# First expert product packed by depth, in pairs of blocks

## What is computed

```python
scores = einsum('bsd,de->bse', x, gate_w) + gate_b        # 4 experts
probs = softmax(scores); masked = top-2 of probs, renormalised
h = gelu(einsum('bsd,edh->ebsh', x, w1) + b1)             # 96 -> 384 per expert, exact gelu
y = einsum('ebsh,ehd->ebsd', h, w2) + b2                  # 384 -> 96
out = einsum('bse,ebsd->bsd', masked, y)
x = x + out
```

## Time and profile before

| | us |
|---|---|
| median of 3 runs | 454.79 |
| the runs | 450.12, 454.79, 462.21 |
| span of the profiled execution | 451.7 |
| its own device time | not given; only its span is |
| PE busy | 406.7 (90%) |
| ACT busy | 347.4 (77%) |
| DVE busy | 344.2 (76%) |
| POOL busy | 124.6 (28%) |
| experts' stage, first L1422 to the end of the span | 288.6 to 451.7 |

### The profile page before, as it was taken

How to read it: one execution, slowest core, us unless ns; L and a number is a source line. 1 busy time by engine, 2 the same in 40 slices (tenths; PEclk the granted TensorE clock), 3 DMA queues, 4 the chain that set the end, 5 groups by cost and what they waited for, 6 DMA issues and landing times.

```text
span 451.7 us, 14565 instructions
## 1 busy us (share of the span) xinstructions
PE 406.7 (90%) x5198; PEld 311.8 (69%) x5198; DVE 344.2 (76%) x983; ACT 347.4 (77%) x920; POOL 124.6 (28%) x300
## 2 busy tenths in 40 slices
PE   4658799999999887999999988879999999999995
PEld 2346577777777765777777766668856777777773
DVE  3858788898888976788778886475677877777775
ACT  3548989899899875899999988446786777777773
POOL 5013234434434313334343335186020000000000
PEclk9999999999999999899999998579999999999999
DMA  7310000000000000000000000022002211311300
GB/s 208 73 59 2 2 2 0 0 0 0 0 0 0 2 3 1 3 4 0 0 0 0 0 1 2 1 80 63 0 19 75 87 53 36 89 39 49 87 17 17
DMA packets 7781, 12.15 MB, mean 27 GB/s; under 512 B 2099, under 2 KB 6601, under 8 KB 6982
## 3 DMA queue, kind: packets, MB, share of 16 engines
q1 hardware_dynamic: 7386, 11.60, 9.1%
q0 software_dynamic: 96, 0.07, 0.2%
q10 hardware_dynamic: 268, 0.08, 0.1%
HBM read 10.06 MB, written 1.68 MB: 26 GB/s over the span
## 4 chain that ended last, share of the span: by engine, by line
PE 45%; DVE 27%; ACT 14%; issue 10%; DMA 2%; DVEq 1%; POOL 0%; ACTq 0%; POOLq 0%
PE score_banks L1436 4%; PE score_banks L1433 4%; PE score_banks L1434 4%; DVE negmax L941 3%; PE score_banks L1422 3%; PE score_banks L1423 3%; PE score_banks L1424 3%; ACT qT L898 3%; PE bank L764 2%; ACT kT L899 2%; DVE sumsq L994 2%; PE bank L752 2%; PE score_banks L707 2%; PE bank L810 2%; PE bank L785 2%
## 5 line engine op out<-in xcount | busy, mean ns | idle before, releaser
L1585 DVE TENSOR_TENSOR hidden_lo<-hidden,hidden_hi 128x512 fp32r<-128x512 f32 x96 | 65.7, 686 | 22.6 <-ACT hidden_hi L1489 22.5
L1097 POOL TENSOR_TENSOR stack<-qk,ones 128x192 f16<-128x192 f32 x64 | 32.4, 506 | 152.2 <-DVE qk L1017 84.0
L1487 ACT ACTIVATE hidden<-score_banks 128x512 f32<-128x512 f32 x64 | 38.4, 599 | 24.6 <-PE score_banks L1424 18.8
L752 PEld LDWEIGHTS bank<-vals,probsT 128*64 128x64 f32 (+1 forms) x1536 | 35.1, 126 | 15.0 <-issue 13.3
L820 PE MATMUL score_banks<-perm,probs 128*128 128x128 f32 x288 | 42.5, 275 | 1.6 <-ACT probs L888 1.6
L764 PE MATMUL bank<-w_qkv,xnT 128*128 128x192 f32 x128 | 39.7, 393 | 4.3 <-DVE qk L1017 2.6
L752 PE MATMUL bank<-vals,probsT 128*64 128x18 f32 (+1 forms) x1536 | 41.4, 208 | 1.1 <-DVE x_all L981 0.6
L1436 PE MATMUL score_banks<-hidden_lo,w_hi 128*96 128x512 f32 x96 | 39.0, 406 | 1.9 <-DVE hidden_lo L1585 1.7
L1433 PE MATMUL score_banks<-hidden_hi,w_hi 128*96 128x512 f32 x96 | 39.3, 409 | 0.6 <-ACT hidden_hi L1489 0.6
L1434 PE MATMUL score_banks<-hidden_hi,w_lo 128*96 128x512 f32 x96 | 38.4, 400 | 0.0
L1489 ACT ACTIVATE hidden_hi<-score_banks 128x512 fp32r<-128x512 f32 x64 | 38.0, 593 | 0.0
(11 more groups left out here) (193 smaller groups left out, 1015.7 us busy)
## 6 DMA issues: line engine op xcount, KB each, us to landing
xT_all<-gate_scratch SPq DMA_DIRECT2D x8, 768.0 KB, 5.1
x_all<-in_x SPq DMA_DIRECT2D x4, 384.0 KB, 7.5
out<-moe_final SPq DMA_DIRECT2D x8, 192.0 KB, 2.0
w<-in_w SPq DMA_DIRECT2D x1, 579.0 KB
w<-in_w SPq DMA_DIRECT2D x1, 576.0 KB, 5.3
w_qkv<-in_w_qkv SPq DMA_DIRECT2D x2, 144.0 KB, 6.8
perm<-in_permutations SPq DMA_DIRECT2D x1, 256.0 KB, 2.8
bias_f<-col_scratch SPq DMA_DIRECT2D x8, 12.0 KB
```

The costliest lines, as they stand in the source:

```text
L752: last = pe.matmul(o_bank[rows, pair_of[h2] * 2 * vd:(pair_of[h2] + 1) * 2 * vd], probsT[:, h2, rows], buffer_of(k, odd, -1)[:, w, pair_of ...
L1487: nc.scalar.activation(hidden[m % 2][:], h_bank[m % HBUF], ACT.Gelu)
L1585: v.tensor_tensor(hidden_lo[m % HBUF][:], hidden[m % 2][:], hidden_hi[m % HBUF][:], ALU.subtract).then_inc(q["hidden_lo"], 1)
```

## The change

The three products of a block together sum over 288 rows (96 channels times hi.hi, hi.lo, lo.hi). They are now laid out as two matmuls of 128 rows and a rest of 32 rows. The tiles w1_a, w1_b, w1_c and x_a, x_b, x_c hold the parts stacked on 128 partitions; DMAs between SBUF tiles fill partitions 96 to 127 (pack_weights once, pack_input and pack_last for each chunk, all on SP's queue). Blocks go in pairs: four matmuls of 128 rows, then the two rests, one on partitions 64 to 95 and one on 96 to 127, into two PSUM banks, then pe_second of the two blocks of the pair before. The bias b1 moves from the 97th row into the GELU's bias operand. There are four hidden banks. DVE's steps are put in a new order by hand (dve_first_chunk, dve_chunk): the accumulation of expert 2 moves into the next chunk, the inputs' subtractions come after dve_low of the same block. The transposed gates get a PSUM place of their own, inputs use bank 2 from chunk 1 on, small result tiles now lie in the memory of w1 and w2, and PE's program is straight code for all chunks.

```diff
@@ build: tiles
-        w1_hi, w1_lo = (sb("w1_" + n, [K1, EXPERTS * HID], F32R) for n in ("hi", "lo"))
+        w1_a, w1_b, w1_c = (sb("w1_" + n, [P, EXPERTS * HID], F32R) for n in "abc")
-        moe_hi, moe_lo = (sb("moe_" + n, [K1, CHUNKS, CHUNK], F32R) for n in ("hi", "lo"))
+        moe_a, moe_b = (sb("moe_" + n, [P, CHUNKS, CHUNK], F32R) for n in "ab")
+        moe_c = sb("moe_c", [P, 2, CHUNK], F32R)
@@ experts
-    HBUF = 3
-    LAG = 2
+    HBUF = 4
+    PAIRS = NH // 2
+    THIRD = C // 3
-    h_bank = [score_banks[0][:, 0, :], score_banks[0][:, 1, :], bank[3][:]]
+    h_bank = [score_banks[0][:, 0, :], score_banks[0][:, 1, :], bank[0][:], bank[3][:]]
-    x_bank = [bank[0], bank[2]] + [bank[0]] * (CHUNKS - 2)
+    x_bank = [bank[0]] + [bank[2]] * (CHUNKS - 1)
+    gates_T_ps = g_bank[:, P:2 * P]
     def pe_first(pe, c, m):
-        w = slice(m * P, (m + 1) * P)
-        pe.matmul(h_bank[m % HBUF], w1_hi[:, w], xT_hi[:, c, :], start=True, stop=False)
-        pe.matmul(h_bank[m % HBUF], w1_hi[:, w], xT_lo[:, c, :], start=False, stop=False)
-        pe.matmul(h_bank[m % HBUF], w1_lo[:, w], xT_hi[:, c, :], start=False, stop=True).then_inc(q["hidden_ps"], 1)
+        w, h = slice(m * P, (m + 1) * P), h_bank[m % HBUF]
+        pe.matmul(h, w1_a[:, w], x_a[:, c, :], start=True, stop=False, skip_group_check=True)
+        pe.matmul(h, w1_b[:, w], x_b[:, c, :], start=False, stop=False, skip_group_check=True)
+
+    def pe_rest(pe, c, j):
+
+        for m, x, first in ((2 * j, x_a[:, c, :], 2 * THIRD), (2 * j + 1, x_c[:, c % 2, :], 3 * THIRD)):
+            rows, w = slice(first, first + THIRD), slice(m * P, (m + 1) * P)
+            pe.matmul(h_bank[m % HBUF], w1_c[rows, w], x[rows, :], start=False, stop=True,
+                      skip_group_check=True).then_inc(q["hidden_ps"], 1)
     def pe_chunk(pe, c, k, tail=None, attention_done=None):
-        for m in range(NH):
-            ...
+        for j in range(PAIRS):
+            if j == 0:
+                pe.wait_ge(q["x_packed"], PACKS * (c + 1))
+                pe.wait_ge(x_last_packed[c % 2], 16 * (c // 2 + 1))
+            if is_chunk(c, 0) and j == 0:
+                tail(0)
+            pe_first(pe, c, 2 * j)
+            if is_chunk(c, 0) and j == 0:
+                tail(1)
+            if is_chunk(c, 0) and j == 1:
+                pe_second(pe, 0, 0)
+                pe.wait_ge(attention_done, B)
+            pe_first(pe, c, 2 * j + 1)
+            pe_rest(pe, c, j)
+            if is_chunk(c, 0) and j == 0:
+                tail(2)
+            if inputs_at(c, j) is not None:
+                pe_inputs(pe, inputs_at(c, j))
+            if gates_at(c, j) is not None:
+                pe_gates(pe, gates_at(c, j))
+            if j == 2 and not is_chunk(c, 0):
+                pe_output(pe, c - 1, 1 - k)
+            if is_chunk(c, 1) and j == 5:
+                pe_gates_T(pe, 1)
+            for m in (2 * j - 2, 2 * j - 1):
+                if m >= 0 and not (is_chunk(c, 0) and m == 0):
+                    pe_second(pe, c, m)
+                elif m < 0 and not is_chunk(c, 0):
+                    pe_second(pe, c - 1, NH + m)
+            if is_chunk(c, 0) and j == 1:
+                pe_gates_T(pe, 0)
     def act_chunk(act, c, k):
-            nc.scalar.activation(hidden[m % 2][:], h_bank[m % HBUF], ACT.Gelu)
+            nc.scalar.activation(hidden[m % 2][:], h_bank[m % HBUF], ACT.Gelu, bias=b1_cols[:, m:m + 1])
             at_least(act, q["hidden_used"], G + 1 - HBUF)
-            nc.scalar.activation(hidden_hi[m % HBUF][:], h_bank[m % HBUF], ACT.Gelu).then_inc(q["hidden_hi"], 1)
+            nc.scalar.activation(hidden_hi[m % HBUF][:], h_bank[m % HBUF], ACT.Gelu,
+                                 bias=b1_cols[:, m:m + 1]).then_inc(q["hidden_hi"], 1)
...
+    def pack_weights(sp):
+
+        sp.wait_ge(s["layers"][0]["q"]["w1_split"], 1 + MIDDLE)
+        wa, wb, wc = (w[:].bitcast(F32) for w in (w1_a, w1_b, w1_c))
+        sp.dma_start(wb[0:C, :], wa[0:C, :]).then_inc(q["w1_packed"], 16)
+        sp.dma_start(wb[C:P, :], wc[0:THIRD, :]).then_inc(q["w1_packed"], 16)
+        sp.dma_start(wa[C:P, :], wc[THIRD:2 * THIRD, :]).then_inc(q["w1_packed"], 16)
+        sp.dma_start(wc[C:P, :], wc[2 * THIRD:C, :]).then_inc(q["w1_packed"], 16)
+
+    def pack_input(sp, c):
+
+        sp.wait_ge(q["xhi_ready"], c + 1)
+        at_least(sp, q["x_packed"], PACKS * c)
+        high = x_a[:].bitcast(F32)
+        sp.dma_start(x_b[:].bitcast(F32)[C:P, c, :], high[0:THIRD, c, :]).then_inc(q["x_packed"], 16)
+        sp.dma_start(high[C:P, c, :], high[THIRD:2 * THIRD, c, :]).then_inc(q["x_packed"], 16)
+
+    def pack_last(sp, c, k):
+
+        at_least(sp, q["hidden_ps"], NH * (c - 1))
+        sp.dma_start(x_c[:].bitcast(F32)[C:P, k, :],
+                     x_a[:].bitcast(F32)[2 * THIRD:C, c, :]).then_inc(x_last_packed[k], 16)
+
     def sync_program(sp):
+        pack_weights(sp)
+        for c in range(2):
+            pack_input(sp, c)
+            pack_last(sp, c, c)
         store_gates(sp, 0)
         load_spread(sp, 0, 0)
         load_spread(sp, 1, 1)
+        for c in range(2, CHUNKS):
+            pack_input(sp, c)
+        pack_last(sp, 2, 0)
         store_output(sp, 0, 0)
         store_gates(sp, 1)
         load_spread(sp, 2, 0)
+        pack_last(sp, 3, 1)
...
     def pe_program(pe, tail, attention_done):
-        pe.wait_ge(s["w1_loaded"], 16 * 2)
+        pe.wait_ge(q["w1_packed"], 16 * 4)
         pe_chunk(pe, 0, 0, tail, attention_done)
-        for c in range(1, 4):
+        pe_chunk(pe, 1, 1)
+        for c in range(2, CHUNKS):
             pe_chunk(pe, c, c % 2)
-        with pe.Fori(2, CHUNKS // 2) as cc:
-            pe_chunk(pe, 2 * cc, 0)
-            pe_chunk(pe, 2 * cc + 1, 1)
-        for m in range(NH - LAG, NH):
+        for m in range(NH - 2, NH):
             pe_second(pe, CHUNKS - 1, m)
         pe_output(pe, CHUNKS - 1, 1)
```

More of the change, by code:

```diff
@@ L128, in build @@
         layers = [attention(nc, sb, sem, s, layer) for layer in range(2)]
+        s["layers"] = layers
         whole_program(nc, s, setup, layers, experts(nc, sb, sem, s, out))
@@ L665, in attention @@
              "stat_ready", "ln_step", "ln_logged", "ln_guessed", "ln_newton_step", "w1_split", "w2_split")
-    q = {n: sem(n + L) for n in names}
+    only = (("xn_ready", "xnT_ps", "ln_step", "ln_logged", "ln_guessed", "ln_newton_step"),
+            ("squares_ready", "squares_summed", "sumsq_ready", "log_ready", "guess_ready", "newton_step", "rnorm_ready",
+             "row_group_done", "probsT_copied_b", "w1_split", "w2_split"))
+    q = {n: sem(n + L) for n in names if n not in only[layer]}
     def on(n):
@@ L1344, in experts @@
     xT = s["moe_xT"]
-    weighted = sb("moe_weighted", [C, CHUNK])
-    acc = [sb(f"acc{k}", [C, CHUNK]) for k in range(2)]
-    final = [sb(f"moe_final{k}", [P, CT, C]) for k in range(2)]
+    weighted = s["w1"][:, 0:CHUNK]
+    acc = [s["w1"][:, (1 + k) * CHUNK:(2 + k) * CHUNK] for k in range(2)]
+    final = [s["w2"][:, k * CT:(k + 1) * CT, :] for k in range(2)]
     gates = sb("gates", [P, UNITS, EXPERTS])
@@ L1373, in experts @@
     q = {n: sem("moe_" + n) for n in names}
+    x_last_packed = [sem(f"moe_x_last_packed{k}") for k in range(2)]
     spread_loaded = [sem(f"moe_spread_loaded{k}") for k in range(2)]
@@ L1376, in experts, with inputs_at, gates_at @@
     GSTEPS = 7
-    def inputs_at(c, m):
-        if is_chunk(c, 0) and m in (2, 4, 6, 8, 10):
-            return 1 + m // 2
-        return 7 if is_chunk(c, 1) and m == 0 else None
-    def gates_at(c, m):
-        if is_chunk(c, 0) and m in (4, 6, 8, 10):
-            return m // 2
-        return {0: 6, 2: 7}.get(m) if is_chunk(c, 1) else None
+    PACKS = 16 * 2
+    def inputs_at(c, j):
+        if is_chunk(c, 0) and j > 0:
+            return 1 + j
+        return 7 if is_chunk(c, 1) and j == 0 else None
+    def gates_at(c, j):
+        if is_chunk(c, 0) and j > 1:
+            return j
+        return {0: 6, 1: 7}.get(j) if is_chunk(c, 1) else None
     def pe_inputs(pe, c):
@@ new lines, in dve_first_chunk @@
+    def dve_first_chunk(v, last_statistics):
+        dve_low(v, 0, 0)
+        last_statistics()
+        rank_first(v)
+        dve_low(v, 0, 1)
+        dve_select(v, 0)
+        dve_renormalise(v, 0)
+        dve_low(v, 0, 2)
+        dve_inputs(v, 2)
+        dve_gates_T(v, 0)
+        dve_low(v, 0, 3)
+        dve_low(v, 0, 4)
+        dve_inputs(v, 3)
+        dve_low(v, 0, 5)
+        norm_root(v, s, q, 1)
+        dve_low(v, 0, 6)
+        dve_inputs(v, 4)
+        dve_weigh(v, 0, 0, 0)
+        dve_low(v, 0, 7)
+        dve_low(v, 0, 8)
+        dve_inputs(v, 5)
+        dve_weigh(v, 0, 0, 1)
+        dve_low(v, 0, 9)
+        dve_accumulate(v, 0, 0, 1)
+        dve_low(v, 0, 10)
+        dve_inputs(v, 6)
+        dve_weigh(v, 0, 0, 2)
+        dve_low(v, 0, 11)
@@ new lines, in dve_chunk @@
+    def dve_chunk(v, c, k):
+        dve_accumulate(v, c - 1, 1 - k, 2)
```

(36 more changed lines are left out.)

106 lines of the change are left out of this document (24 added, 82 removed).

## The result

The changed kernel took **459.13 us** (median of 21 runs, 456.65 to 470.22), the kernel before 455.83 (21 runs, 449.73 to 466.47). The ratio is 1.0123, with a 95% interval of 1.0088 to 1.0158: a little over one per cent slower. Ratios here are taken without the slow executions, those more than 1.5% above the fastest of their kernel; the two medians alone would give 1.007. Two later measurements of the same changed kernel gave 1.0064 [1.0027, 1.0101] and 1.0152 [1.0087, 1.0217].

The account below looks back on a forecast made before the run. PE's matmuls were taken to bound the steady chunks. Pairs +5.8, tail +0.3, chunk 0 -0.7 and chunk 1 -0.7 gave +4.7 on a 451.7 us span, 456.4; 3.1 from span to median made 459.5 us, range 455 to 464.

Parts of the forecast that it names:

- Price of a visit (Part 1): PE, one pair of blocks: layout changes and open weight loads make it 2.90 us against 2.79 before.
- Its effect on a chunk: PE in the experts' chunks: +0.12 us for each of 48 pairs, +5.8 us in all; steady chunks about 17.9 us.
- Loads not ahead: PE at layout changes: the first weight load after one lies open, 0.10 us for the rests, 0.08 for the second product.
- Rival 2: PE pairs: array empties at layout changes but weight loads run ahead; 2.71 us a pair, total 449.9 us; chance 0.12.
- Rests beside each other: PE, end of each pair's first products: both 32-row rests run at once, streaming in 0.21 us together.
- Rival 3: PE pairs: the two rests don't overlap; +10.2 us on top of the forecast's +5.8, total 469.7 us; chance 0.10.
- Rival 1: PE pairs: changing row groups alone costs nothing; 2.56 us a pair, total 444.6 us; chance 0.10.
- ACT and the bias (Part 3): ACT's GELUs: even 0.1 us more each for the bias would hide in 0.31 us idle a block; nothing added.
- Chunk 0: First experts' chunk: three second-product matmuls fall into the 2.00 us wait for the gates, -0.7 us.
- Chunk 1: Second experts' chunk: PE waits for DVE, so the slower PE (6 x 0.12) falls into those waits, -0.7 us.
- rival 4: Chunks 0 to 2: layout changes as forecast plus a wait of 4 to 8 us; total 464 to 468 us; chance 0.07.
- Tail: After the last pair: second products wait for the odd block's low part, ending about 0.5 us late against 0.2, +0.3 us.

Follow-up runs that it names:

- again: The changed kernel measured once more without any edit, beside the kernel before: 459.71 us, ratio 1.0064 to the kernel before.
- no bias: The changed kernel with the bias operand left out of its GELUs, so b1 is missing from the result: 460.92 us in a single run.
- full_rests: The changed kernel with both rests of a pair issued as 128-row matmuls, leaving no layout change (wrong products added): 454.24 us, 0.9971 of the kernel before.
- third profile of the kernel before: The kernel before, unedited, profiled again as the second of two extra runs: 450.59 us.
- the first form of the triples: The changed kernel with blocks in threes, three rests on three row groups: 455.29 us, 1.0069 of the kernel before; later form, gates spread: 452.08 us, 0.9963.

## Why the prediction was right, and where it was not

The total was right: 459.5 predicted, 459.13 measured, and the forecast's mechanism holds in the steady chunks. But the sum has terms that were off, and several of the faults offset each other.

- **Price of a visit (Part 1): right.** Last packed matmul to rests: 0.31 forecast, 0.318 or 0.319 in 43 of the 48 pairs of "again" (two ran at half clock, three took 0.33). Rests to the next: 0.42 against 0.423 to 0.431 at full clock. That one to its follower: 0.31 against 0.307 to 0.314. Pair: 2.90 against 2.907. The prices were read from changes of layout in the attention layers and the setup, of other shapes and types, and carried over within 0.01 us.
- **Its effect on a chunk: 0.62 us, not 0.72.** A pair took 2.794 us before and takes 2.907: +0.113, where I took +0.12. The one pair of a chunk that holds the output transposes took 3.15 before and takes 3.21, only +0.06: before, the first step behind the transposes lasted 0.315 us in place of 0.233, and in the changed kernel that step is one of the 0.31 that are paid anyway. Over eight chunks this is +5.0 us against the +5.8 forecast.
- **Loads not ahead: right.** Rival 2 would have given 2.71 us a pair. The load of L1439 starts with its matmul, as the one of L707 does in the earlier trace rows. The rule behind that rival (the Trainium skill, "TensorE: Matmul & The Clock Gate", Step-by-step) does not describe this trace across a change of layout; inside one layout it does, as the load at 401.10 shows. The Trainium skill, "TensorEngine Tiling (Array Packing)", Key Properties, says that a change of tiling mode drains the array; the 0.32 us before the rests, where 0.23 is the step inside one layout, agree.
- **Rests beside each other: right.** They start 3 to 4 ns apart; on one row group they cost 0.237 us a pair more. Rival 3 is refuted. It was priced at +10.2 (48 x 0.21 is 10.1); the pairs of the kernel on one row group give 11.4, its total +8.0 (467.72 against 459.71 beside it), as chunk 1 took some of it back. Rival 1 is refuted too: a change of row groups alone costs 0.09 us here (0.318 against 0.227), as much as those that move columns.
- **ACT and the bias (Part 3): nothing, as forecast,** but its idle before a pair is 0.48 us and not 0.8: each GELU starts 0.08 us later after the one before it, four to a pair. The Trainium skill, "ScalarE: Activation LUTs", What ACT_TABLE_LOAD costs, gives about 93 ns for a per-partition bias operand; the traces have 689 ns with it ("again") and 602 to 607 without ("no bias"), 82 to 87 ns. The packing transfers and the unrolled code cost nothing in the steady chunks, as full_rests shows.
- **Chunk 0: right in its length, not in its terms.** Six pairs at +0.12 and -0.7 for the second product inside the gates' wait were to cancel; measured 26.9 us against 26.9 and 27.2. But PE is idle for 0.36 us in it ("again") against 2.41 (26.93 - 24.52), 2.05 less and not 0.7, since the wait for hidden_lo ahead of the gates went too (0.64 us before); and it runs at a clock of 0.85 against 0.91, which takes back about 1.6 us (an estimate: 0.15 x 26.9 against 0.09 x 26.9). That the length agrees is luck. Against the execution that I summed on it is 3.4 us less, since that chunk 0 held an extra stretch at half clock. I saw its mean clock of 0.81 and took it for the stage's own.
- **Chunk 1: wrong.** The forecast had again 0 (+0.7 for the pairs, -0.7 in waits for DVE). Measured +2.2 to +2.4: the kernel waits 2.91 us for the gates, ahead of second products that were ready, and runs 3.4 us at half clock behind that. The step that failed is that "the slower PE falls into those waits": a wait of this kind in chunks 0 to 2 was rival 4, and part of it came true. The waits for hidden_lo that I meant did vanish; the one for the gates grew, from 0.25 us to 2.91. What I hadn't seen in the change is that the transpose of the second gates, which stood behind the second product of block 9, now stands in front of the last pair's two second products, those of blocks 8 and 9. With it moved behind them the chunk takes 22.06 us, 0.3 under before, and the forecast for it holds.
- **Tail: +0.45, where +0.3 was forecast.** From the last chunk's first matmul to the end it is 24.3 us in three profiles of the kernel before and 25.4 in two of the changed kernel, 0.62 of it the chunk's own; "again" has 25.7, with the clock at half for its last 4.5 us in place of 1.1 to 1.2. Ahead of the last but one block's third matmul PE waits 0.33 us for hidden_lo, where it waited 0.14, and ahead of the output transposes 1.70 us for DVE, where it waited 1.56. The remaining 0.1 I didn't take apart.
- **Start of the experts' stage: +1.8 us, not forecast.** It starts at 287.9 to 288.7 in three profiles of the kernel before and at 290.4 and 290.5 in "again" and its repetition. The difference arises between 34 and 60 us, where nothing of the first product runs. Windows of that stretch, the changed kernel ("again") first and the kernel before (its third profile) second:
```profile
34.40:60.00 25.60, 22.41 (x307) 17.55 (x307) 19.97 (x66) 21.45 (x65) 6.67 (x17) 0.93 0.01 2
```
```profile
34.40:60.00 25.60, 20.92 (x370) 16.15 (x370) 20.99 (x72) 23.20 (x70) 7.28 (x19) 1.00 0.01 2
```
In the same 25.6 us the changed kernel issues 307 matmuls, the kernel before 370. The 0.93 is only the 3.4 us at half clock from 56.5 us; the view counts the time ahead of the first entry of the clock's record, here 39.45 us, as full. That this time was at half speed too is seen in six equal matmuls, of "again" first and of the third profile of the kernel before second:
```profile
35.56 1.49 PE L828 MATMUL score_banks<-perm,probs 128*128 128x128 f32 x6
```
```profile
35.63 0.82 PE L820 MATMUL score_banks<-perm,probs 128*128 128x128 f32 x6
```
Set side by side, "again" falls behind by 1.2 us over the first of the two stretches and by 1.1 over the second. The clock's first lasting rise comes at 33.5 to 34.4 us in the three profiles of the kernel before and at 35.5 us or later in all ten that carry the change. The one at 35.5 is the first form of the triples, which has the change's edits ahead of the experts too. It lies 1.0 us behind the third profile of the kernel before from its first matmuls on and keeps that distance, its clock rises at the same place in the work within 0.1 us, it has the same full clock from 34.4 to 60 us, and its stage starts at 289.8 us:
```profile
34.40:60.00 25.60, 21.02 (x347) 15.59 (x345) 20.57 (x71) 23.25 (x69) 6.70 (x17) 1.00 0.01 2
```
So the later start is time at half clock, and not work that the change adds. Why the other nine rise later is **open**: no experiment isolated it, and three profiles of the kernel before are few to tell it from chance.

Added up between "again" (span 456.9) and the third profile of the kernel before (448.8): start +1.8, chunk 0 -0.25, chunk 1 +2.2, chunk 2 +0.5, chunks 3 to 6 +2.5, last chunk and tail +1.4, together +8.1. That is above the measured ratio (+0.9 to +1.6%, 4 to 7 us), because this profile of the kernel before is one of its fastest executions (450.59 us, where the 21 runs begin at 449.73 and have their median at 455.83). Against the execution that the prediction used, with the 3.2 to 3.4 us that its chunk 0 lost to the clock, the difference is 5.2 us, close to the forecast's 4.7. So the forecast left out +2.2 in chunk 1, +1.8 at the start and +0.5 in the tail (0.35 of it clock), had 0.8 too much in the pairs, and summed on a base with over 3 us of clock in it that didn't come again. It also added 3.1 us from span to time, where every run here has about 1.8 between the two; the other 1.3 were a guess at how far that execution lay under the median. That these nearly cancel is luck; what was foresight is the price of a visit, the overlap of the rests, and that ACT would hide the bias.

## What to carry to other kernels

Packing the rest of a contraction onto row groups saves matmuls, and each visit to the row groups has a fixed price, here 0.32 + 0.43 + 0.31 us in place of three steps of 0.23: about 0.37 us beyond what else is streamed, whether it holds two rests or three (one row group each). Count the 512-column steps saved per visit (0.23 us each) against it: one saved per visit lost 0.14 us a visit; two saved should gain 0.09, and 16.91 - 4 x 0.09 = 16.55 us a chunk is what the triples gave (16.59). When a loop is regrouped, look at every operation with a foreign producer (here the gates' transpose) and keep it behind the work that is ready, because the new grouping may have put it in front.
